# A residual stack of a quantiser and three linear stages: the first weight stage as rounded products over feature halves, with the operands rounded and split by four engines and queues

## Time and profile before

| what | us |
|---|---|
| median of three runs | 486.75 |
| lowest, highest of the three | 483.95, 487.24 |
| span of the profiled execution, first to last instruction | 481.9 |
| TensorE busy | 464.9 (96%) |
| VectorE busy | 419.4 (87%) |
| ScalarE busy | 358.6 (74%) |
| GpSimd busy | 45.5 (9%) |

### The profile page before, as it was taken

One profiled execution on the slowest core, in us unless ns is written; L12 is line 12 of the kernel. 1 busy time (PEld: TensorE's weight loads), 2 busy tenths in 40 slices (PEclk: granted clock), 3 DMA queues, 4 the chain that ended last, 5 costly groups with the idle time before them and its releaser, 6 DMA issues.

```text
span 481.9 us, 8215 instructions
## 1 busy us (share of the span) xinstructions
PE 464.9 (96%) x3184; PEld 424.7 (88%) x3184; DVE 419.4 (87%) x481; ACT 358.6 (74%) x383; POOL 45.5 (9%) x46
## 2 busy tenths in 40 slices
PE   3999869999999999999999999999999999999997
PEld 3969669898999989898999989898999989898995
DVE  5999999999999899989999899989999899989120
ACT  6979958678877879678877879678887879675011
POOL 1064000200002000200002000210003000100000
PEclk9999989999999999999999999999999999999999
DMA  7997214712335122712335122712335122702002
GB/s 282 407 415 258 113 34 149 294 54 97 131 127 212 44 95 97 294 44 103 131 120 218 44 89 101 294 44 103 131 101 237 44 86 104 294 2 88 1 1 87
DMA packets 17830, 67.07 MB, mean 139 GB/s; under 512 B 2576, under 2 KB 5904, under 8 KB 13712
## 3 DMA queue, kind: packets, MB, share of 16 engines
q1 hardware_dynamic: 17808, 66.81, 37.9%
HBM read 56.84 MB, written 9.96 MB: 139 GB/s over the span
## 4 chain that ended last, share of the span: by engine, by line
PE 90%; ACT 3%; DMA 3%; DVE 2%; issue 1%; POOL 1%; SPq 0%; DVEq 0%
PE x_bank L603 45%; PE acc L628 34%; PE acc L579 3%; PE x_bank L616 3%; PE acc L640 2%; PE acc L638 2%; DMA w1b<-w 2%; DMA rows<-own_rows 1%; ACT mask L344 1%; ACT w2h L400 1%; DVE y L460 1%; PE acc L567 1%; ACT tq L329 1%; PE acc L577 0%; ACT outb L404 0%
## 5 line engine op out<-in xcount | busy, mean ns | idle before, releaser
L603 PEld LDWEIGHTS x_bank<-x,w1b 128*128 128x128 f32 x2048 | 233.2, 193 | 8.2 <-issue 4.9
L603 PE MATMUL x_bank<-x,w1b 128*128 128x128 f32 x2048 | 234.8, 276 | 3.7 <-DVE x L475 3.7
L344 ACT ACTIVATE mask<-absx,negtop 128x1024 bf16<-128x1024 f32 x112 | 128.4, 1146 | 40.3 <-DVE y L460 39.5
L329 ACT ACTIVATE tq<-xin,magic,rdelta 128x1024 f32<-128x1024 f32 x128 | 157.0, 1234 | 0.6 <-DVE yhigh L526 0.3
L460 DVE COPY_PREDICATED y<-mask,uq 128x1024 f32<-128x1024 int16 x112 | 151.1, 1349 | 0.1
L439 DVE TENSOR_SCALAR tq<-tq,par 128x1024 f32<-128x1024 f32 x128 | 99.2, 775 | 3.7 <-DVE y L460 3.1
L448 DVE TENSOR_SCALAR uq<-tq,ylow,yhigh 128x1024 f32<-128x1024 f32 x112 | 92.3, 824 | 0.2 <-DVE y L460 0.2
L628 PE MATMUL acc<-w2h,x2h 128*128 128x512 f32 x256 | 80.9, 393 | 2.0 <-DVE x2l L481 2.0
L628 PE MATMUL acc<-w2h,x2l 128*128 128x512 f32 x256 | 79.9, 390 | 0.0
L628 PE MATMUL acc<-w2l,x2h 128*128 128x512 f32 x256 | 79.2, 390 | 0.0
L295 POOL TENSOR_TENSOR w1b<-w1b,eye 128x256 f32<-128x256 f32 x32 | 36.5, 1140 | 368.9 <-DMA w1b<-w 368.9
(11 more groups left out here) (57 smaller groups left out, 218.9 us busy)
## 6 DMA issues: line engine op xcount, KB each, us to landing
w1b<-w SPq DMA_DIRECT2D x32, 1024.0 KB, 6.7
xin<-x SPq DMA_DIRECT2D x16, 512.0 KB, 3.7
out<-outb SPq DMA_DIRECT2D x14, 512.0 KB, 2.8
w1b<-w2n SPq DMA_DIRECT2D x4, 1024.0 KB, 10.6
ring<-w2t SPq DMA_DIRECT2D x6, 512.0 KB, 6.7
ua<-e_dram SPq DMA_DIRECT2D x16, 128.0 KB, 2.5
ua<-w2t SPq DMA_DIRECT2D x2, 512.0 KB, 7.8
va<-la SPq DMA_DIRECT2D x8, 128.0 KB, 2.7
```

Source lines behind the costliest of these rows:

```text
L329: nc.scalar.activation(tq[:, n % TQ, :], flat(xin, c % UN), ACT.Identity, bias=magic[:, 0:1], scale=rdelta[:, g:g + 1]).then_inc(t_ready, 1)
L344: nc.scalar.activation(mask[:, n % MK, :], absx[:, :], ACT.Relu, bias=negtop[:, g:g + 1], scale=1.0).then_inc(mask_ready, 1)
L603: last = nc.tensor.matmul(x2_bank[2 * t + i][:, o % HALF * P:(o % HALF + 1) * P], w1b[:, o, at:at + P], x1[:, t, k, :], start=(o % HALF == ...
```

## The change

- The quantiser's units are now 512 features of all 256 tokens (still 128 x 1024 elements). A unit h of batch b is features half h.
- W1 of batches 1 to 7 is no longer a full float32 product. Both operands are split into a rounded float32r part and a float32r remainder, and three products are made (W1h.x1h, W1l.x1h, W1h.x1l) with 256 moving columns each, plus the identity times x1h and x1l on the diagonal. For one half h of the contraction that is `w1_half(b, h)`: 4 pieces j, each of 2 output tiles x 3 x 4 matmuls, plus 8 with the identity, 104 in all. Results of both halves gather in four PSUM banks `x2_bank[j]`.
- W1's rounding is done by the DMA: GpSimd issues a DMA that casts the piece (512 KB) into the rounded slot, ScalarE writes its negative into the other slot (`negate_w1`), and GpSimd issues a second, accumulating DMA of the same data onto it, which leaves the remainder. 8 pieces per batch, each loaded twice, in a ring of 4 (`w1s`). The low-rank factor u is made in the same way (`round_u`, `negate_u`, `u_remainder`).
- x1 is summed by VectorE in place in `xin`, rounded by ScalarE (`round_x1`, 128 x 1024), and split by VectorE (`split_x1`, 128 x 1024). `DIRECT` holds all units from batch 1 on, so `sum_x1` and GpSimd's `round_x1` issue nothing.
- The order on TensorE for a batch b >= 1: w1_half(b, 1), product(0), v_x2, w1_half(b+1, 0), u_low for t=0, product(1), u_low for t=1. The x2 banks are rounded and split one after another (`ACT_BANK`, `DVE_BANK`). The low-rank result has its rounding and split at steps 31 and 30 (`ACT_LOW`, `DVE_LOW`), and w1_half(b+1, 0) waits for it before its piece j=2.
- `ycut` has its own buffer. Batch 0 keeps the full float32 W1 product; its W1 loads no longer wait for `g_tiles`, since W2's table copy lies in other memory. ScalarE copies the identity to float32r (`eye_r`) before its first step. All loops are unrolled.

```diff
+    HC = HALF * P
+    SLOT = (0, 2, 1, 3)
+    DIRECT = tuple(range(UN, UN * B))
...
+        x1 = under("x1", [P, UN, KT, P])
+        x1h = sb("x1h", [P, UN, HALF, T], f32r)
+        stage_x = under("stage_x", [P, 2, D])
+        x1l = sb("x1l", [P, UN, HALF, T], f32r)
+        x2h = sb("x2h", [P, KT, T], f32r)
+        x2l = sb("x2l", [P, KT, T], f32r)
         outb = sb("outb", [P, UN, D])
-        w1b = sb("w1b", [P, OT, D])
+        w1b = under("w1b", [P, 2, OT, HC])
+        w1s = sb("w1s", [P, PAIRS, 2, D], f32r)
...
+        def x1_adds(c):
+
+            return min(c + 1, UN) + sum(d <= c for d in DIRECT)
+
+        def x1_sums(c):
+
+            return c + 1 - x1_adds(c)
+
+        def x1h_made(c):
+
+            direct = len([d for d in DIRECT if d <= c and d % UN == c % UN])
+            if c in DIRECT:
+                return x1h_ready[c % UN], direct
+            return x1h_in[c % UN], 16 * (c // UN - direct)
...
-                sp.wait_ge(g_tiles, 2 * (j + 1))
...
+            for b in range(1, B):
+                if b < LAST:
+                    a, lab = ids_of(b + 1)
+                    sp.wait_ge(x1l_ready[0], b)
+                    load_x(b + 1, 0)
+                    sp.wait_ge(vl_ready, 2 * (b + 1))
+                    load_v(a, lab)
+                store(b - 1, 0)
+                if b < LAST:
+                    sp.wait_ge(x1l_ready[1], b)
+                    load_x(b + 1, 1)
+                store(b - 1, 1)
...
+            def round_u(b):
+                if b:
+                    pool.wait_ge(acc_done, ACCS * b)
+                else:
+                    pool.wait_ge(w2l_ready, ST + 2)
+                    nc.gpsimd.memset(u_hh[:, :].bitcast(f32), 0.0).then_inc(u_pads, 1)
+                    nc.gpsimd.memset(u_hl[:, :].bitcast(f32), 0.0).then_inc(u_pads, 1)
+                    pool.wait_ge(u_pads, 2)
+                    pool.wait_ge(e_out, 16 * EH)
+                for into, r in ((u_hh, 0), (u_hh, DUP), (u_hl, 0)):
+                    for lo, hi, rows_of in u_rows(adapter[b]):
+                        nc.gpsimd.dma_start(into[r + lo:r + hi, :], rows_of).then_inc(u_in, 16)
+
+            def u_remainder(b):
+
+                pool.wait_ge(u_negated, b + 1)
+                for lo, hi, rows_of in u_rows(adapter[b]):
+                    nc.gpsimd.dma_start(u_hl[DUP + lo:DUP + hi, :], rows_of.bitcast(f32r), accum_op=ALU.add) \
+                        .then_inc(ul_in, 16)
+
+            def w1_item(b, h, j):
+                return w1[bass.ds(adapter[b], 1), h, :, 2 * j:2 * j + 2, :].rearrange("a p j n -> (a p) (j n)")
+
+            def round_w1(b, h, j):
+                m = item(b, h, j)
+                if m < PAIRS:
+                    pool.wait_ge(w1_used, 2 * (j // 2) + 2)
+                else:
+                    pool.wait_ge(item_used, m - PAIRS + 1)
+                nc.gpsimd.dma_start(w1s[:, SLOT[j], 0, :], w1_item(b, h, j)).then_inc(h_in[j], 16)
+
+            def w1_remainder(b, h, j):
+
+                pool.wait_ge(h_negated, item(b, h, j) + 1)
+                nc.gpsimd.dma_start(w1s[:, SLOT[j], 1, :], w1_item(b, h, j).bitcast(f32r), accum_op=ALU.add) \
+                    .then_inc(l_in[j], 16)
...
+            for c in range(UN, UN * B):
+                b, h = divmod(c, UN)
+                if h:
+                    round_u(b)
+                if c + 1 < UN * B:
+                    nb, nh = divmod(c + 1, UN)
+                    if nh == 0:
+                        adapter[nb] = pool.value_load(ids_a[0:1, nb:nb + 1], min_val=0, max_val=NA - 1)
+                    round_w1(nb, nh, 0)
+                    round_w1(nb, nh, 1)
+                    round_w1(nb, nh, 2)
+                    w1_remainder(nb, nh, 0)
+                    round_w1(nb, nh, 3)
+                    w1_remainder(nb, nh, 1)
+                    sum_x1(c + 1)
+                    w1_remainder(nb, nh, 2)
+                    w1_remainder(nb, nh, 3)
+                    round_x1(c + 1)
+                if h:
+                    u_remainder(b)
...
+        ACT_BANK, DVE_BANK = (23, 24, 25, 26), (22, 23, 24, 25)
+        ACT_NEG = (25, 26, 27, 28)
+        ACT_X1, DVE_X1 = 12, (11, 12)
 
         ACT_V, DVE_V = 14, 15
-        ACT_U, DVE_U = 21, 23
-        ACT_LOW, DVE_LOW = 26, 27
-        ACT_OUT = (30, 30, 31, 32)
-        END = STEPS + PER + 1
+        ACT_U = 29
+        ACT_LOW, DVE_LOW = 31, 30
+        ACT_LOW0, DVE_LOW0 = 26, 27
+        ACT_OUT = (35, 35, 39, 39)
+        END = STEPS + 2 * PER
...
+            def round_bank(b, j):
+                act.wait_ge(item_used, item(b, 1, j) + 1)
+                nc.scalar.activation(x2h[:, 2 * j:2 * j + 2, :].rearrange("p k t -> p (k t)"), x2_bank[j][:, :],
+                                     ACT.Copy).then_inc(x2h_ready, 1)
+
+            def negate_w1(b, h, j):
+                m = item(b, h, j)
+                act.wait_ge(h_in[j], 16 * (m // PAIRS + 1))
+                nc.scalar.activation(w1s[:, SLOT[j], 1, :], w1s[:, SLOT[j], 0, :].bitcast(f32), ACT.Copy, scale=-1.0) \
+                    .then_inc(h_negated, 1)
+
+            def round_x1(c):
+                b, h = divmod(c, UN)
+                act.wait_ge(x1_ready, x1_adds(c))
+                if b == 1:
+                    act.wait_ge(w1_used, PAIRS)
+                else:
+                    act.wait_ge(item_used, item(b - 1, h, PAIRS))
+                nc.scalar.activation(x1h[:, h, :, :].rearrange("p k t -> p (k t)"), xin[:, h, :], ACT.Copy) \
+                    .then_inc(x1h_ready[h], 1)
...
+            act.wait_ge(b_in, 64)
+            nc.scalar.activation(eye_r[:, :], eye[:, :], ACT.Copy).then_inc(eye_ready, 1)
...
+                for c in DIRECT:
+                    if n == G * c + ACT_X1:
+                        round_x1(c)
                 for b in range(B):
                     s = n - PER * b
                     if s == ACT_V:
                         round_v(b)
...
+                    for j in range(PAIRS):
+                        if b and s == ACT_BANK[j]:
+                            round_bank(b, j)
+                        if b and s == ACT_NEG[j] - G:
+                            negate_w1(b, 1, j)
+                        if b < LAST and s == ACT_NEG[j]:
+                            negate_w1(b + 1, 0, j)
+                    if s == ACT_U:
+                        negate_u(b)
+                    if s == (ACT_LOW if b else ACT_LOW0):
...
-                if n % G == 1 and n >= G:
-                    dve.wait_ge(x1_ready, n // G)
...
+            def split_x1(c):
+                b, h = divmod(c, UN)
+                dve.wait_ge(*x1h_made(c))
+                nc.vector.tensor_tensor(x1l[:, h, :, :].rearrange("p k t -> p (k t)"), xin[:, h, :],
+                                        x1h[:, h, :, :].rearrange("p k t -> p (k t)").bitcast(f32),
+                                        ALU.subtract).then_inc(x1l_ready[h], 1)
...
+                for b in range(1, B):
+                    for j in range(PAIRS):
+                        if n == PER * b + DVE_BANK[j]:
+                            split_bank(b, j)
+                for c in range(UN, UN * B):
+                    if n == G * c + DVE_X1[0 if c in DIRECT else 1]:
+                        split_x1(c)
...
+            def w1_half(b, h):
+
+                pe.wait_ge(*x1h_made(UN * b + h))
+                if b == 1:
+                    pe.wait_ge(eye_ready, 1)
+                for j in range(PAIRS):
+                    pe.wait_ge(l_in[j], 16 * (UN * (b - 1) + h + 1))
+                    if h == 0 and j == 2:
+                        pe.wait_ge(lowl_ready, b)
+                    for o in (2 * j, 2 * j + 1):
+                        into = x2_bank[j][:, o % 2 * T:(o % 2 + 1) * T]
+                        for part, xs in ((0, x1h), (1, x1h), (0, x1l)):
+                            if j == 0 and xs is x1l and o == 0:
+                                pe.wait_ge(x1l_ready[h], b)
+                            for k in range(HALF):
+                                at = o % 2 * HC + ((k - o) % HALF if o // HALF == h else k) * P
+                                last = nc.tensor.matmul(into, w1s[:, SLOT[j], part, at:at + P], xs[:, h, k, :],
+                                                        start=(h == 0 and o % 2 == 0 and part == 0 and xs is x1h
+                                                               and k == 0),
+                                                        stop=False, skip_group_check=True)
+                        if o // HALF == h:
+                            for xs in (x1h, x1l):
+                                last = nc.tensor.matmul(into, eye_r[:, :], xs[:, h, o % HALF, :], start=False,
+                                                        stop=False, skip_group_check=True)
+                    last.then_inc(item_used, 1)
...
+                w1_half(1, 0)
+                for q in range(ACCS):
+                    u_low(0, q)
+
+            def batch(b):
```

(82 more changed lines are left out.)

282 lines of the change are left out of this document (121 added, 161 removed).

## The result

The changed kernel takes 543.24 us (median of 4 runs, 542.56 to 543.94) against 486.96 before in the same comparison: ratio 1.1186, interval 1.1143 to 1.1228. It is 12% slower. The forecast was 530.9 with a range of 500 to 560: sign and place are right, the size is 12.3 us short.

A forecast was written before the change was run, and what follows sets the result against it. TensorE was taken to bound the kernel before by a small margin; after it, three engines need 50 to 51 us per batch, plus waits. 117 + 6 x 59.3 + 51.5 + 1.7 = 526.0, plus 4.85 gives 530.9 us, range 500 to 560.

The forecast's parts named there:

- my 4.85: Added to the forecast span of 526.0 us: the median of the runs lies 4.85 us above the profiled span.
- up to the 33rd step: First batch, to the start of the kernel's 33rd step: 117 us, where it was 118.2 before.
- six batches: Steady batches: 6 x 59.3 us, from VectorE's 50.7 of work, 8.3 of waits and 0.3 for GpSimd.
- the end: From the last unit's closing step on, product(0) behind that unit: 51.5 us, plus 1.7 for TensorE's lower clock.
- the waits at the banks: VectorE waiting for ScalarE at three of four banks: about 0.4 us each, 1.3 per batch.
- The waits before the x1 split: VectorE waiting for ScalarE's rounding of x1 after ycut: 2.7 us in odd units, 1.7 in even ones.
- Low's wait: VectorE at step 30 waiting for ScalarE's mask and two low copies: at least 2.1 us, taken as 2.6.
- rival 4: TensorE's matmuls with identity or changing weights cost more than 0.1175 us, say 0.145: 534 us; chance within the forecast's 0.60.
- Rival 1: ScalarE is never behind in the steady batches: 55.3 us per batch, 507 us in all; chance 0.17.
- Rival 2: GpSimd's DMAs come late or stretch VectorE: 5 to 10 us more per batch, 560 to 590 us; chance 0.13.
- My 22 us of slack per piece: W1's loads: a piece is freed 22 us before its slot is used again, so DMAs are tight but not late.
- Rival 3: Waits behind absx and low vanish in idle times: 51.6 us per batch, 478 us in all; chance 0.10.

The follow-up runs named there:

- e1: Changed kernel with ScalarE's rounding of x1 one step earlier (ACT_X1 from 12 to 11): 529.5 us, ratio 1.0894 to the kernel before.
- e2: Changed kernel with ScalarE's rounding of low one step earlier (ACT_LOW from 31 to 30): 526.25 us, ratio 1.0835 to the kernel before.
- e3: Changed kernel without the product of W1's remainder with rounded x1 in batches 1 to 7, 64 matmuls fewer per batch: 538.43 us, ratio 1.1077.
- e12: e10 with ScalarE's negation of u moved from step 29 to step 26, in front of absx: 487.9 us, ratio 1.0044 to the kernel before.
- e7: Changed kernel with the edits of e1 and e2, output copies a step or more earlier and bank roundings ahead of negations: 502.74 us, ratio 1.0363.
- e10: e7 with the ring of masks 3 deep in place of 2: 496.98 us, ratio 1.0242 to the kernel before.
- e5: Changed kernel without W1's accumulating DMAs, TensorE taking the negated rounded part as remainder: 542.09 us, ratio 1.1195 to the kernel before.
- e9: Changed kernel with the ring of masks 3 deep in place of 2, nothing else: 530.71 us, ratio 1.0949 to the kernel before.
- e11: e7 without ScalarE's negations of W1 from the second half of batch 1 on: 487.06 us, ratio 1.0036 to the kernel before.
- e8: e7 without W1's accumulating DMAs, the edit of e5: 502.13 us, ratio 1.0342 to the kernel before.

## Why the prediction was right, and where its size was off

Its sum had three terms, and each can be read in the trace. Before and after, the kernel's 33rd step starts at this row of VectorE's timeline of the changed kernel, there:

```profile
119.94 0.75 DVE L572 TENSOR_SCALAR tq<-tq,par 128x1024 f32<-128x1024 f32 x1 [0.57 <-DVE y L591]
```

Six periods are taken as six times the distance of two lows over five, and the end is what is left of the span.

| term | forecast | measured | off by |
|---|---|---|---|
| up to the 33rd step | 117 | 119.9 | +2.9 |
| six batches | 6 x 59.3 = 355.8 | 6 x 61.58 = 369.5 | +13.7 |
| the end | 51.5 + 1.7 = 53.2 | 52.7 | -0.5 |
| span | 526.0 | 542.1 | +16.1 |

The median of 543.24 is only 1.1 above this span, where I had added 4.85; that gives 3.7 us back, and leaves the 12.3 that forecast and median differ by. This is luck: every run on record whose span is known is 1.7 to 2.0 above it (543.94 against 542.1). The span of 481.9 before fits only the shortest of the three runs, 483.95, and my 4.85 compared it with their median. Without it the forecast would have been some 15 us short.

**The term that was mis-sized is the waits at the banks.** "Three of four banks ... about 0.4 each, 1.3" measured 1.32 + 0.35 + 1.30 = 2.97. I had seen the outputs at step 35 (they are in the walk to the x1 split) but not that those at step 39 are step 23 of the next batch, the step of bank 0, and that the loop writes the negation of step 25 ahead of bank 2. One us of output copies and one of negation, each in a step where VectorE already waits, are two waits of 1 us. This is 1.67 of the 2.28 us that a batch is off. The rest: VectorE's work with its own y 51.5 against 51.0 (50.7 and the 0.3 for GpSimd), low 2.89 against 2.6, the x1 splits 0.19 less. The sum is 1.67 + 0.51 + 0.29 - 0.19 = 2.28.

**Right, and shown by runs:**
- The waits before the x1 split, 2.59 and 1.62 where 2.7 and 1.7 were walked through; the odd unit's is one pair of output copies longer. e1 took them away.
- Low's wait, released by ScalarE, and worth its full price: e2 took away 2.66 per batch and 17.0 in all.
- TensorE isn't the bound (e3). Its cost per matmul is the 0.12 that v_x2 had shown, within 2%, so rival 4 has no case. It works 54.5 us per batch (108.94 / 2, the window being two batches) and not 50.0: two starts at the lower clock, 469.60 to 477.90 for 56 matmuls and 480.82 to 487.98 for 48, cost 1.6 and 1.4 over 0.12 each; a further 0.5 is the 0.12 against my 0.1175, and about 1 us of the 4.5 is not traced. I had charged the clock once, at the end; in the steady batches it fills idle time, so it cost nothing there.
- The end: TensorE alone, with product(0) behind the last unit. 52.7 us against 37.7 before (481.9 less 118.17 and 6 x 54.33). This part has nothing to do with waits, and it decides e12: 116.55 to the 33rd step, 6 x 53.0 and 51.2 make its 485.8. It saves 1.6 at the start and 7.9 in the batches, and pays 13.5 at the end.

**Rival 1** (507, ScalarE never behind) needed another order; e7 and e10 come near it, with batches of 54.2 to 55.8 where it said 55.3, and take 503 and 497. **Rival 2** is refuted by e5 for the changed kernel: neither of its signs is in its steady batches. My 22 us of slack per piece is measured nowhere, but the loads were late by little: 2.5 us of TensorE's waits in six batches, at a share of 0.82. In faster batches it comes into sight. ScalarE waits for DMAs at its negations in e7, e9, e10 and e12 (in e12 five times before 440 us, 2.1 us in all), and the loads of W1 are 6% of e7's last chain and 8% of e10's. The Trainium skill's page "SBUF — State Buffer", section "SBUF: two separate sides", would have had GpSimd locked out of the port pair that the two share, and the loads late, while VectorE runs in a mode that holds it. No row here names the mode of VectorE's operations; if they are in it, it didn't reach the changed kernel's time: 16 GpSimd issues of W1 per batch cost no more than 8, and VectorE's 758 and 827 ns are not above what e5 has. **Rival 3** put its point at 53 us per batch, where "the result equals before". e11 and e12 reached 53.0 and came out 0.4% above it, which bears out both the point and that the result there is level.

The 33rd step came 1.8 us later than before (119.94 against 118.17), where I had put it 1.2 earlier. ScalarE's timeline of the changed kernel at its start:

```profile
8.52 0.31 ACT L530 ACTIVATE eye_r<-eye 128x128 fp32r<-128x128 f32 x1 [2.80 <-DMA rows<-own_rows]
8.74 2.36 ACT L433 ACTIVATE tq<-xin,magic,rdelta 128x1024 f32<-128x1024 f32 x2
```

Its first tq begins at 8.74 where it was 6.01, 2.7 late, where I had allowed 2. At the low of batch 0 0.75 of that is left (98.67 against 97.92), and 1.0 more comes up to the 33rd step, with the first x1 split waiting 2.71 us in it. Which part of my allowance was wrong there is not shown.

## What to carry to other kernels

When work moves from the bound engine to two others that run in lockstep, add up their busy times first, then walk through every step of the order in which one waits for the other: here 2.97 + 4.21 + 2.89 us of waits a batch, each of which moves with one or two instructions of 1 us, turned 51.5 us of work into 61.6. List every instruction of the slower partner by its step modulo the batch, since a step number of the previous batch falls on one of this; and put work that nobody waits for where that engine waits itself (e12: one instruction, 9 us). When the waits are gone, look at the loads again: what had slack in a batch of 61.6 us was late at times in one of 55 (e7 and e8). Taking one such wait away gives only part of it back if the next one has no slack (e1: 4.2 removed, 2.1 gained), and a deeper ring doesn't help behind a step that both must pass (e9).
